# An activated FFN layer laid out token by token in place of channel by channel, in a one-block vision transformer

## The reference, cut to what matters

```python
def act_quant(x):
    scale = 127.0 / jnp.clip(jnp.max(jnp.abs(x), axis=-1, keepdims=True), 1e-05)
    return jnp.clip(jnp.round(x * scale), -128, 127) / scale
...
h = bit_linear(x, w1)                                  # 256 -> 1024 channels
h = depthwise_conv1d(h.transpose(0, 2, 1), conv_w, conv_b)   # three taps along the tokens
h = jax.nn.silu(h.transpose(0, 2, 1))
return bit_linear(h, w2)                               # act_quant(h), then 1024 -> 256
```

## Time and profile before

| | |
|---|---|
| Median of three timed runs | 191.03 us (190.18 to 192.08) |
| Span of the profiled execution, first to last instruction | 188.4 us, 2.6 us under that median |
| VectorE busy in it | 133.4 us (71%), 265 instructions |
| TensorE busy, matmuls and weight loads | 133.7 and 108.2 us |
| ScalarE, GpSimd busy | 80.7 us, 86.2 us |
| Mean granted clock of TensorE | 0.882 of full speed |

### The profile page before, as it was taken

One profiled execution on the slowest core, in us unless ns is written; L12 is line 12 of the kernel. 1 busy time (PEld: TensorE's weight loads), 2 busy tenths in 40 slices (PEclk: granted clock), 3 DMA queues, 4 the chain that ended last, 5 costly groups with the idle time before them and its releaser, 6 DMA issues. The chain is left out here.

```text
span 188.4 us, 2077 instructions
## 1 busy us (share of the span) xinstructions
PE 133.7 (71%) x672; PEld 108.2 (57%) x672; DVE 133.4 (71%) x265; ACT 80.7 (43%) x137; POOL 86.2 (46%) x97
## 2 busy tenths in 40 slices
PE   0596989895786999977994595894499249407620
PEld 0585758674564688965673573892499139307410
DVE  0142132069878499777599999779989999698930
ACT  3277250229204523651860464595257355711200
POOL 4000108997239460346172597719192460091900
PEclk9999999999699999996999998599659955855996
DMA  6997993000000000000000000001000001000011
GB/s 191 249 267 220 373 247 95 0 0 0 0 0 3 3 0 0 3 0 2 0 0 0 0 0 0 3 2 43 22 0 0 0 12 61 3 0 0 7 59 56
DMA packets 4226, 9.05 MB, mean 48 GB/s; under 512 B 570, under 2 KB 3000, under 8 KB 4088
## 3 DMA queue, kind: packets, MB, share of 16 engines
q1 hardware_dynamic: 4216, 8.93, 16.5%
HBM read 7.71 MB, written 1.21 MB: 47 GB/s over the span
## 5 line engine op out<-in xcount | busy, mean ns | idle before, releaser
L465 PE MATMUL pair<-linT,xT 128*111 128x256 f32 (+1 forms) x132 | 33.2, 410 | 4.8 <-ACT xT L656 3.4
L465 PEld LDWEIGHTS pair<-linT,xT 128*111 128x111 f32 (+1 forms) x132 | 24.4, 189 | 11.7 <-ACT xT L656 3.6
L386 POOL TENSOR_TENSOR z<-x_flat,s_row 128x666 f32<-128x666 f32 (+1 forms) x12 | 17.9, 1524 | 18.7 <-ACT s_row L734 18.7
L693 ACT ACTIVATE y<-pair,cb_sb,cw_sb 128x333 f32<-128x333 f32 (+2 forms) x32 | 17.4, 597 | 16.4 <-PE pair L507 16.3
L507 PE MATMUL pair<-xq_hi,w1T 128*128 128x334 f32 (+2 forms) x64 | 18.6, 381 | 3.2 <-DVE xq_lo L901 2.3
L321 POOL TENSOR_TENSOR rstd<-var,minus_half 111x3 f32<-111x3 f32 x8 | 7.8, 974 | 21.9 <-DVE var L838 21.9
L507 PE MATMUL pair<-xq_lo,w1T 128*128 128x334 f32 (+2 forms) x64 | 17.0, 353 | 0.0
L913 DVE SCALAR_TENSOR_TENSOR y<-pair,cw_sb,y 128x324 f32<-128x324 f32 (+2 forms) x32 | 15.1, 509 | 2.2 <-ACT x_flat L704 1.6
L825 DVE TENSOR_TENSOR h<-pair,pos_sb 111x256 f32<-111x256 f32 (+1 forms) x11 | 4.4, 400 | 17.1 <-PE pair L465 17.1
L507 PEld LDWEIGHTS pair<-xq_hi,w1T 128*128 128x128 f32 x64 | 13.7, 246 | 4.3 <-DVE xq_lo L901 2.6
L861 DVE RECIPROCAL krec<-ksum 128x333 f32<-128x333 f32 (+2 forms) x8 | 15.8, 1980 | 0.0
(11 more groups left out here) (112 smaller groups left out, 277.3 us busy)
## 6 DMA issues: line engine op xcount, KB each, us to landing
x_flat<-in_x_dram SPq DMA_DIRECT2D x6, 576.0 KB, 11.3
out_dram<-o_sb SPq DMA_DIRECT2D x10, 111.0 KB
z<-in_L_ffn_w_dram SPq DMA_DIRECT2D x1, 1024.0 KB, 7.1
y<-in_L_ffn_w_dram SPq DMA_DIRECT2D x1, 1024.0 KB, 10.4
lin_sb<-in_L_tok_W_lin_dram SPq DMA_DIRECT2D x1, 768.0 KB, 5.2
wk_sb<-in_L_attn_Wk_dram SPq DMA_DIRECT2D x1, 256.0 KB, 10.4
wv_sb<-in_L_attn_Wv_dram SPq DMA_DIRECT2D x1, 256.0 KB, 10.5
wq_sb<-in_L_attn_Wq_dram SPq DMA_DIRECT2D x1, 256.0 KB, 10.1
```

The lines of the kernel that those rows point to most:

```text
L386: nc.gpsimd.tensor_tensor(z_of[f][:, 2 * i:2 * i + 2, :], act_of[f][:, 2 * i:2 * i + 2, :], s_row[:, :T[f]].unsqueeze(1).to_broadcast([P, ...
L465: last = nc.tensor.matmul(ps[:n, j % 2, :D], xT[:, k, FIRST[g] * L + t0:FIRST[g] * L + t0 + n], linT[:, k, :], start=(k == 0), stop=(k == ...
L693: nc.scalar.activation(y(f)[:, k, :], pair(("f1", f, i))[:, b, :T[f]], ACT.Identity, bias=cb_sb[:, k:k + 1], scale=cw_sb[:, k, 1:2]).then_ ...
```

## The change

act_of keeps its shape in the code, 128 x 8 x T, and changes its place in memory. Before, a chunk's tokens lie side by side and the chunks follow each other (333 words apart in groups 0 to 2, 222 in group 3). After, the 8 words of one token lie side by side, and the next word of the same chunk is 8 words (32 bytes) on. y, z, q2 and the order of all instructions are the same, and so are the waits.

```diff
--- before.py
+++ after.py
@@ -163,7 +163,11 @@
 
         y_flat = sb("y", [P, KH * TM])
         y = channels("y", KH, fp32, y_flat[:, :], TM)
-        act_h = channels("act_h", KH, fp32, x_flat[:, 2 * KD * TM:(2 * KD + KH) * TM], TM)
+        def token_rows(at):
+
+            return lambda g: at[:, :KH * T[g]].rearrange("p (t k) -> p k t", k=KH)
+
+        act_h = token_rows(x_flat[:, 2 * KD * TM:(2 * KD + KH) * TM])
         hmax = sb("hmax", [P, TM])
 
         hmax_a = kv_sb(SIZES.index(max(SIZES)))[:, 0, :]
@@ -183,8 +187,9 @@
 
         spare = xT[:, :, :].rearrange("p k t -> p (k t)")
         last = [spare[:, i * KH * TM:(i + 1) * KH * TM] for i in range(2)] + [spare[:, 2 * KH * TM:2 * KH * TM + KH * TM // 2]]
-        act_of, z_of, q2_of = ([buf(g) for g in range(G - 1)] + [channels("", KH, dt, at)(G - 1)] for buf, dt, at in (
-            (act_h, fp32, last[0]), (z, fp32, last[1]), (q2, bf16, last[2])))
+        act_of = [act_h(g) for g in range(G - 1)] + [token_rows(last[0])(G - 1)]
+        z_of, q2_of = ([buf(g) for g in range(G - 1)] + [channels("", KH, dt, at)(G - 1)] for buf, dt, at in (
+            (z, fp32, last[1]), (q2, bf16, last[2])))
 
 
         pairs = [ctx.enter_context(nc.psum_tensor(f"pair{i}", [P, 2, BANK], fp32)) for i in range(NPAIR)]
```

## The result

The changed kernel took 194.9 us (median of four runs), the kernel before 190.75 us beside it: ratio 1.0162, interval 1.0107 to 1.0218. Timed again with twelve runs in another session it took 193.6 against 191.44, ratio 1.012 (1.008 to 1.0161). Medians are over all executions, and a ratio is that of the faster of the two states in which each kernel's executions come. So the changed kernel is 1.2 to 1.6% slower, by the ratios 2.3 and 3.1 us, by the medians 2.2 and 4.2. The forecast was 4.5 us slower, 195.5.

What follows compares the result with a forecast made beforehand. VectorE, with a second chain through ScalarE, GpSimd and TensorE nearly as late in steps g = 2 and 3, was taken as the bound. Terms of 4.7 - 0.1 - 0.9 + 0.8 = +4.5 us gave 195.5 us, range 188.5 to 198.5.

Steps and rivals of the forecast that it cites:

- the prediction's own sign for that: Silu and maxima: the forecast is wrong in its path if L713 is long and L951 doesn't move.
- the sum: Whole kernel, step by step: 4.7 - 0.1 - 0.9 + 0.8 = +4.5 us, added to the median of 191.03.
- the fourth quantise: Step g = 3: VectorE's fourth L972 waits 0.5 us for GpSimd's longer multiplies, bringing the delay to +4.7 us.
- the end: Group 3: half maxima -0.65 and -0.25 us, join of the halves left unchanged, L962 +0.8 us.
- Step g = 2 ... L951 is at 105.1 instead of 102.94: +2.2: Step g = 2: longer Silu delays token scaling, embedding and transposes, so L951 comes 2.2 us later; the wait eats the reduce's gain.
- The convolution's +1.0: Group 0's convolution, step g = 1: longer tap copies let through 0.3 and 0.7 us, so +1.0 us.
- from 133.09 to 137.3: +4.2: Step g = 3: Silu ends 5.8 us later, the maxima's transposes follow, and L951 moves 4.2 us later.
- the join (L945: Joining group 3's half maxima: 1.53 us for 222 words, held by something beside it; left unchanged, bounds -1.1 to +0.6 us.
- The spread write costs nothing: Rival on ScalarE's writes: L656's extra comes from its short rows, so the kernel gains 3.7 us, 187.3 us; chance 0.13.
- 0.6 ns a word: Rival: ScalarE's spread writes cost what VectorE pays for reading; 191.4 us, no change; chance 0.18.
- more than the sum: Rival: lower TensorE clock, GpSimd's reads at the upper bound, or a reduce that doesn't shorten; 198 to 200 us; chance 0.11.

Runs made afterwards that it cites:

- reads alone: Kernel before, with GpSimd's multiply and tap addition reading words 8 apart from a constant tensor: ratio 1.0238, 195.92 us against 191.81.
- The single parts: Kernel before with only the maxima's reads, only ScalarE's writes or only GpSimd's reads in the new layout: ratios 0.9697, 1.0209 and 1.0238.
- the writes alone: Kernel before, with ScalarE writing words 8 apart and every reader reading a constant tensor channel by channel: ratio 1.0209, 195.46 us against 191.81.
- the kernel before with the new order: Kernel before, with group 3's scales ahead of group 2's first two quantise instructions and its row transposes ahead of the first down-projection chunks: ratio 1.0108, 193.14 us.

## Why the prediction came out where it did

The sign was right, the size too large (4.5 against 2.3 and 3.1 us), and the path was wrong by the prediction's own sign for that: L713 is long, and L951 didn't move to later in the steps g = 2 and 3. That the sum came near is luck. L951 of step g = 3 was 4.6 us off to one side, and the fourth quantise and the end, with 1.1 and 3.4 us that the sum didn't have, to the other.

**Prices.** The maxima were forecast at 2.6, 2.9, 1.5 and 1.1 us and took 2.62, 2.93, 1.53 and 1.08. GpSimd's reads were taken at 0.8 ns a word and cost 0.77 (reads alone). L962 was to get 0.8 us longer and got 0.84 longer; but on the way to the DMA that the end follows stand GpSimd's two multiplies of group 3, which have no term in the sum and got 1.1 us longer. ScalarE's writes were taken at 1.19 ns a word from L656 and cost (1420 - 754) / 666 = 1.00; and as instructions behind each other overlap, four of them cost 2.08 and 2.36 us where the sum had 2.8 and 3.2. ScalarE's busy time rose by 9.5 us where some 14 were forecast.

**"Step g = 2 ... L951 is at 105.1 instead of 102.94: +2.2" failed.** It moved by -0.6. Three things were mis-sized. The convolution's +1.0 was +0.34 at the start of Silu. Silu gave 2.08 and not 2.8. And GpSimd's rounding behind it was carried on with its old 2.41 us; it took 1.40. Before, the first of its three instructions took 1.48 us, beside a scan of VectorE (L855), and now 0.48; so a microsecond of the old duration had been waiting, and the embedding moved by 1.3 us, not 3.8. In step g = 3, "from 133.09 to 137.3: +4.2" failed with it: -0.4. So the reduce's gain paid for the longer Silu, with 0.6 and 0.4 us over. The single parts agree: the writes alone do cost 4.0 us, where the long reduce still follows the late Silu.

**"VectorE's fourth quantise ... waits 0.5" was mis-sized.** Counted from the tap copy the four ended 1.2 us later than before and had stood at -0.4 ahead of them, so 1.6. The four multiplies took 9.28 us, where 6.21 + 2.1 was the forecast: the price of the reads was right, and the fourth got another microsecond longer with three quantise instructions in it.

**The quantise of group 2 at the end is not in the prediction.** It had the multiplies of group 2 end in time and looked there only at the join (L945, left at -1.1 to +0.6; it gave -1.0). Group 2's multiplies still run when VectorE comes to its first two quantise instructions, and these end with one multiply each: 4.35 instead of 0.91, 3.4 us. The spread reads are a part of that only: the two took 3.48 us without them, and with the maxima alone shortened the first of them took 1.66. In these versions VectorE's maxima are short as well; that it comes while GpSimd still multiplies because of that is argued and not shown. The Trainium skill has the rule that would have warned: in "SBUF — State Buffer", section "Who interferes with whom", a VectorE instruction in a two-port mode and a GpSimd instruction exclude each other for the whole of either, and `tensor_scalar` can take such a mode. The trace agrees as far as it goes: 2.21 and 2.22 us beside multiplies of 2.07 and 2.17, 0.5 us without one. Of the 168 quantise instructions of groups 0 to 2 in the fourteen profiles 143 take 0.45 to 0.55 us, and the other 25 all end 0.32 to 0.37 us after an instruction of GpSimd; where quantise comes first, GpSimd's instruction gets longer, as the fourth multiply of step g = 3 with its 3.06 us. That the two keep each other waiting is shown by this. No run here has the quantise in another mode, so that the mode is the cause is argued and not shown.

**The rivals.** "The spread write costs nothing" and "0.6 ns a word" are refuted by Silu's 1.00. In the reserve of "more than the sum" the prediction had GpSimd's reads at their upper bound; the price was the middle one, and what it led to was larger. A lower granted clock of TensorE, in the same reserve, is not where the time went: from L951 of step g = 2 to that of g = 3 it was 0.91 (before 0.89), from there to group 2's 0.69 (0.70). Behind group 3's L951 it was 0.65 (0.84), but there the first output DMA waits for GpSimd.

**Still open.** How much of the loss from the spread reads comes through held-up quantise instructions and how much through late multiplies wasn't timed apart. One pair of profiles, the changed kernel with and without these reads, says where it arises: counted from the tap copy L951 of step g = 3 stands at 53.24 and 53.13, group 2's at 82.86 and 80.15, group 3's at 93.85 and 90.27, and the first of the last five DMAs at 101.23 and 97.07. So 2.6 of the 4.2 us arise between the first two, with the late multiplies and the 1.80 us that VectorE stands idle, 0.9 up to the third, with the two held quantise instructions, and 0.6 behind. And the collisions come and go between versions, as in the kernel before with the new order.

## What to carry to other kernels

A layout has one price for each engine that touches it. Here the one reader that gained 5.8 us alone stood against two engines that lost 4.0 and 4.5 alone; a step of two words, which still gives the reader runs, gave it the same gain at a tenth of the writer's price, and with the next buffer in the same order the kernel is 3.5% faster than before.

A duration in a profile can hold waiting for another engine. Before carrying it along a moved chain, compare the same shape elsewhere in the trace; and where an instruction gets longer on one engine, look for the instructions of other engines that will now run beside it, not only for those that wait for its result. And count up to what the end of the span follows, here the first of the last output DMAs: an order that brought the last arithmetic forward and that DMA back made the kernel slower.

## What the runs showed of the hardware that was not expected

- ScalarE's write of 666 words took 754 ns side by side, 823 two words apart and 1420 eight words apart: the step of two costs 0.10 ns a word, the step of eight 1.00.
- VectorE's fp32 to bf16 quantise of 592 words took 460 ns also where its source stepped two words; no slower form was seen.
- GpSimd's multiply of 666 words took 1477 ns where its broadcast operand repeated each word twice, against 1536 where it ran through the row twice.
- The four quantise instructions of one group took between 1.58 and 3.90 us in versions whose code around them is the same. In fourteen profiles such an instruction either took 0.45 to 0.55 us or ended 0.32 to 0.37 us after an instruction of GpSimd.
- The span ended 10.3 to 10.8 us after the first of the last five output DMAs in all fourteen profiles, however late the others were issued.
